# Attention scores as four quadrants of the matmul array: two heads on the rows, two halves of the queries on the columns

## The reference, cut to what matters

```
h = shift_token(x);  q, k, v = split(h @ wqkv);  q, k = l2norm(q) * qs, l2norm(k) * ksc
q, k = rotary_xpos(q, k)
bq = windows(q) * 8;  bk, bv = [previous window, own window] of k, v      # 128 queries, 256 keys
sim = einsum('bhwid,bhwjd->bhwij', bq, bk)
mask = (i < j) | (i > j + 128) | (j == -1)   # i, j: positions of query and key
out = softmax(where(mask, -max, sim)) @ bv;  x = x + out @ wo
```

## Time and profile before

| | |
|---|---|
| median of 3 runs | 977.15 us (977.08 to 978.51) |
| the profiled execution | 977.5 us, span 975.8 us |
| granted TensorE clock, mean | 0.993 |
| TensorE busy | 912.9 us (94%), 5688 matmuls |
| VectorE busy | 676.0 us (69%) |
| ScalarE busy | 514.0 us (53%) |
| GpSimd busy | 425.7 us (44%) |
| L1913, the scores, matmuls of 256 columns | 384, busy 47.9 us |
| L1913, matmuls of 128 columns | 128, busy 9.3 us |

### The profile page before, as it was taken

The page is one execution under the profiler, slowest core; times in us unless marked ns, Lnnn a source line. Parts: engine busy times, 40 slices in busy tenths (PEclk is TensorE's granted clock), DMA queues, the critical chain, the costliest instruction groups (busy, mean ns, idle before and its releaser), DMA issues.

```text
span 975.8 us, 17517 instructions
## 1 busy us (share of the span) xinstructions
PE 912.9 (94%) x5688; PEld 767.4 (79%) x5688; DVE 676.0 (69%) x1706; ACT 514.0 (53%) x1221; POOL 425.7 (44%) x420
## 2 busy tenths in 40 slices
PE   5999987999999969999999799999999999889998
PEld 4778875787878848888888688887888888768887
DVE  6889888476767686776767556677677766746563
ACT  5577830404040436767676634455767666654442
POOL 4432634022220386767676300007776767631110
PEclk9999998999999999999999999999999999999999
DMA  7202021000000000000001020000000000000001
GB/s 259 76 1 65 22 89 69 1 1 0 0 1 1 23 0 2 1 23 0 22 0 35 16 102 14 4 27 1 2 24 0 22 0 21 19 16 16 31 25 47
DMA packets 15716, 26.34 MB, mean 27 GB/s; under 512 B 1642, under 2 KB 12256, under 8 KB 14896
## 3 DMA queue, kind: packets, MB, share of 16 engines
q1 hardware_dynamic: 15664, 25.69, 8.0%
HBM read 20.53 MB, written 2.10 MB: 23 GB/s over the span
## 4 chain that ended last, share of the span: by engine, by line
PE 74%; DVE 11%; ACT 7%; issue 4%; POOL 3%; SPq 1%; DMA 1%; ACTq 0%; DVEq 0%; POOLq 0%
PE bank L1610 35%; PE bank L1959 5%; PE bank L1913 5%; PE bank L1937 5%; PE bank L1819 5%; PE bank L1923 4%; ACT probs L1477 3%; PE bank L1900 2%; PE bank L1782 2%; PE bank L1765 1%; DVE y L839 1%; DVE normed L1140 1%; PE bank L1947 1%; PE bank L2032 1%; PE bank L2029 1%
## 5 line engine op out<-in xcount | busy, mean ns | idle before, releaser
L1477 ACT ACTIVATE probs<-bank,row_min 128x256 f32<-128x256 f32 (+1 forms) x256 | 110.9, 457 | 119.5 <-DVE row_min L1065 119.5
L1065 DVE CUSTOM_DVE_ANT_0 bank<-bank,mask 128x256 f32<-128x256 f32 (+1 forms) x256 | 90.8, 431 | 5.7 <-PE bank L1913 5.6
L586 POOL TENSOR_TENSOR norms<-norms,minus_half 128x16 f32<-128x16 f32 x32 | 93.6, 2925 | 2.7
L1610 PE MATMUL bank<-wqkv_hi,x_hi 128*128 128x512 f32 x192 | 82.1, 428 | 1.9 <-DVE rot L1041 1.1
L1610 PE MATMUL bank<-wqkv_hi,x_lo 128*128 128x512 f32 x192 | 75.8, 395 | 0.0
L1610 PE MATMUL bank<-wqkv_lo,x_hi 128*128 128x512 f32 x192 | 75.2, 392 | 0.0
L1202 DVE SCALAR_TENSOR_TENSOR hidden<-bank,lcols,hidden 128x512 f32<-128x512 f32 (+1 forms) x48 | 36.0, 750 | 51.4 <-PE bank L1610 26.8
L568 POOL TENSOR_TENSOR q_tok<-rot 128x512 f32<-128x512 f32 x32 | 41.3, 1289 | 58.1 <-DVE rot L1041 58.1
L1923 PE MATMUL bank<-ident,probs 128*128 128x128 f32 x448 | 60.5, 276 | 3.9 <-ACT probs L1477 3.9
L1610 PE MATMUL bank<-t_hi,wm_lo 128*128 128x512 f32 x160 | 63.1, 394 | 0.0
L1959 PE MATMUL bank<-wo_sb,o_t 128*128 128x256 f32 x256 | 60.9, 381 | 2.3 <-DVE o_t L1080 1.7
(11 more groups left out here) (255 smaller groups left out, 2632.3 us busy)
## 6 DMA issues: line engine op xcount, KB each, us to landing
w_stage<-in_wm_l_dram SPq DMA_DIRECT2D x8, 534.0 KB, 3.6
w_stage<-in_wqkv_dram SPq DMA_DIRECT2D x2, 1536.0 KB, 7.7
out_dram<-stream SPq DMA_DIRECT2D x8, 256.0 KB, 2.4
emb<-in_ctx_dram SPq DMA_DIRECT2D x1, 1536.0 KB, 7.0
inner<-in_w_gate_dram SPq DMA_DIRECT2D x1, 1152.0 KB, 10.2
stream<-in_x_dram SPq DMA_DIRECT2D x2, 512.0 KB, 5.7
stream<-in_x_dram SPq DMA_DIRECT2D x1, 1024.0 KB, 12.7
ew<-in_pos_bias_dram SPq DMA_DIRECT2D x1, 1024.0 KB, 11.3
```

What stands on the lines that cost most here:

```text
L586: pool.tensor_tensor(norms[:, 2, :], norms[:, 1, :], minus_half[:, :], ALU.pow).then_inc(c_rn, 1)
L1065: dve.tensor_tensor_reduce(logits, logits, mask[:, 2 * P - nk:2 * P], 1.0, FAR, ALU.add, ALU.min, row_min[:, w % 2, 2 * i + e:2 * i + e + ...
L1477: act.activation(probs[:, i, e, 0:nk], logits, ACT.Exp, bias=row_min[:, w % 2, h:h + 1], scale=-1.0, accum_out=row_sum[:, w % 2, h:h + 1]) ...
L1610: ins = pe.matmul(out, stationary, moving, start=(first and i == 0), stop=(last and i == len(terms) - 1))
```

## The change

In windows with w > 0, each head's score matmul is split into two by queries: g = 0 has queries 0 to 63 as the stationary operand (64 x 64) and keys 0 to 191 as the moving one, and writes partitions 0 to 63; g = 1 has queries 64 to 127 and keys 64 to 255, and writes partitions 64 to 127, 64 columns further right. The two heads stay on the two halves of the array's rows, so the four matmuls of a pair of heads lie on its four quadrants. Places that no quadrant writes keep what the bank held; all of them are masked. In w = 0 windows the matmuls stay as they were. The semaphore is raised where it was. The waits for c_qt and c_pt_out go through `wait_alone`.

```diff
             def score_pairs(n, w):
 
-                pe.wait_ge(c_qt, n + 1)
+                wait_alone(pe, c_qt, n + 1)
                 k0 = max(w - 1, 0) * P
                 nk = (w + 1) * P - k0
                 for i in range(KI):
                     if i % 2 == 0 and not (isinstance(n, int) and n == 0):
-                        pe.wait_ge(c_pt_out, 4 * n - 2 + i)
-                    for e in range(2):
-                        half = slice(e * DH, (e + 1) * DH)
-                        ins = pe.matmul(bank[SCORES[i // 2] + e][:, (i % 2) * 2 * P:(i % 2) * 2 * P + nk],
-                                        q_t[half, i, :], k_t[half, i, k0:(w + 1) * P], start=True, stop=True)
+                        wait_alone(pe, c_pt_out, 4 * n - 2 + i)
+                    for g in range(2 if w else 1):
+                        for e in range(2):
+                            half = slice(e * DH, (e + 1) * DH)
+                            rows_out = slice(g * DH, (g + 1) * DH) if w else slice(0, P)
+                            nq = 3 * DH if w else P
+                            c0 = (i % 2) * 2 * P + g * DH
+                            ins = pe.matmul(bank[SCORES[i // 2] + e][rows_out, c0:c0 + nq], q_t[half, i, rows_out],
+                                            k_t[half, i, k0 + g * DH:k0 + g * DH + nq], start=True, stop=True)
                     if i % 2:
                         ins.then_inc(c_qk, 1)
```

## The result

The changed kernel takes 970.24 us (median of 4 runs, 969.63 to 971.49) against 977.83 for the kernel before in 4 runs of the same comparison: ratio 0.9914, 95% interval 0.9894 to 0.9933. The prediction was 970.0. The profiled execution took 969.63 us, with a span of 967.9, 7.9 us shorter than before.

What follows compares the result with a forecast made beforehand. TensorE was taken to bound the kernel nearly throughout. Per layer 2.76 + 0.50 + 0.20 + 0.08 = 3.54 us, for two layers 7.1, taken off the profiled 977.5 gave 970.4, against the median 970.05; predicted 970.0, range 968.8 to 971.4.

Steps and rivals of the forecast that it cites:

- The sum: Gains over all changed windows: 3.54 us per layer, 7.1 us for two layers.
- G: TensorE time saved in the block of scores per changed window: 1.92 - 1.46 = 0.46 us.
- The bound that had no row: Time of a group of four score matmuls: 0.157 us if all run together, 0.313 if column halves take turns; lower taken.
- Issue: 64 instead of 32 instructions pass TensorE's sequencer; the block wants 46 ns a pair, the trace shows about 20; taken as covered.
- rows 5: Trace rows at the start of layer 2: 16 score pairs within 0.33 us, about 20 ns each.
- The waits set apart: Three waits in the loop made instructions of their own: costed at nothing, range 0 to 0.25 us per window.
- What is late next: Chain from masks to queries' transposes: steady w = 2 and 3 windows gain 0.46 us each, w = 1 0.25.
- A: How much sooner the first half of a window's scores is ready for VectorE's masks: 0.25 us.
- The first and the last batch's w = 1 windows: Gain limited ahead of VectorE's first mask: first batch 0.08 us at most, last batch 0.20.
- The last w = 2 and 3 windows: Last batch, VectorE has other work ahead of the masks: gain 0, waits of 2.55 and 1.24 us grow about 0.46.
- Rivals 1 to 4: 973 us: only A kept (chance 0.13); 977: 59 ns pairs (0.07); 992: halves alternate (0.07); 966: all 24 keep G (0.03).

Runs made afterwards that it cites:

- e1: Kernel before with scores split into four quadrants, each half of the queries still taking all 256 keys; ratio 0.9996 to the kernel before.
- e4: Changed kernel with the two loops swapped, both query halves of one head first; 975.43 us in one run, block of scores 1.46 us.
- e2: Kernel before, unsplit, with 192 key columns instead of 256 in windows with w > 0; ratio 0.9944 to the kernel before.
- e3: Kernel before with only the three waits of the scores set apart as instructions; ratio 1.0004 to the kernel before.
- e6: Changed kernel with the next queries' transposes after all four quarters of the probabilities; 971.91 us, ratio 0.9921 to the kernel before.
- e7: Changed kernel with VectorE's MLP statistics moved after the masks in the last batch's w = 2 window; 970.45 us, ratio 0.9911 to the kernel before.
- e9: Changed kernel with filler matmuls, results unread, in two waits of each layer's last windows; 969.84 us, ratio 0.9914 to the kernel before.
- e8: Changed kernel with the queries' transposes last and VectorE's MLP statistics after the masks; 971.06 us, ratio 0.9907 to the kernel before.
- e5: The changed kernel again, unaltered, on the same chip as three later runs; 971.68 us, ratio 0.9919 to the kernel before.
- e10: Changed kernel with queries' transposes last, MLP statistics after the masks, and filler matmuls in the last windows' waits; 967.61 us, ratio 0.9892 to the kernel before.

## Why the prediction was right

- **The total.** The sum was 7.1 us; measured are 7.6 between the medians and 7.9 between the profiled executions. That 970.0 lies within 0.24 us of the median is partly luck: the sum started from the 977.15 of three runs, and with the fourth the median before is 977.83. These 0.7 us nearly cancel the 0.5 by which the gain was sized too small.
- **G, the block.** Predicted 1.46 us, measured 1.46. The bound that had no row, four quadrants in one group, fell to its lower end: e1 with 256 columns takes 1.89, so four cost what two do, and e4 shows that their order is free. The interpolation by columns holds: e2 measures 0.42 of it alone. (By the prediction's own rows 256 columns come to 2 x 0.83 / 8 = 0.2075 us, not 0.209; that moves the block by less than 0.01.)
- **Issue.** Covered, as rows 5 had said: 32 loads and 32 matmuls in 1.46 us are 46 ns a pair. The 62 ns on a matmul with hardware decode off, which the Trainium skill gives ("TensorE: Matmul & The Clock Gate", section "Wait — 56ns, not 53.3ns?"), are not this kernel's price.
- **The waits set apart.** Free: e3, and no step inside the block.
- **What is late next.** The w = 2 and 3 windows gained G, the w = 1 windows A = 0.25 (measured 0.26), because there the keys' copy still ended last. e6 confirms that by filling the wait, and shows that w = 0 windows hang on it too: a wait that I had passed over, because the listed idle time was small. In the w = 2 windows TensorE stays last, as forecast, but the room behind the keys' copy shrank from 0.51 to 0.42 us and not by G - A = 0.21: the copy begins 6.91 us after the first score instead of 7.32, sooner by 0.41 and not by A. Before the change it began 0.03 after TensorE had ended the keys' transposes, so it followed TensorE there and not ScalarE's chain; timeline of the kernel before, for the earlier trace rows:

```profile
440.65 0.60 PE L1892 MATMUL bank<-ident,k_tok 128*128 128x128 f32 x4
```

  One part of the expected picture was off: TensorE's idle time in the w = 1 windows is 12.38 - 12.23 = 0.15 us, not 0.33. The keys' transposes (L1892) come later as well, 5.51 us after the first score; before the change it was 5.82, less G would be 5.36. They wait for the keys that VectorE scales (L1056), which are done 0.15 us ahead of them (424.60 + 0.68 = 425.28 to 425.43, timeline of the kernel after):

```profile
424.60 0.68 DVE L1056 TENSOR_TENSOR k_tok<-k_tok,norms 128x512 f32<-128x512 f32 x1
```

  The listed end of the matmul before covers that gap.
- **The first and the last batch's w = 1 windows** were sized too small, 0.08 and 0.20 against 0.18 and 0.26. I had bounded them by VectorE's listed idle time; but the first mask starts 0.35 us after x_low's start, inside its listed 0.43 (371.07 and 371.42): listed lengths overlap there, so there was more room than the idle time says. Together that is 0.3 us more gain.
- **The last w = 2 and 3 windows** gained nothing, and their waits grew, as forecast: 2.55 to 3.00. In w = 2, e7 shows that VectorE's statistics ahead of the masks were the reason. What the prediction left out is that in some executions the clock falls at these waits. In the changed kernel's second profile this cost 1.1 and 2.3 us in the last w = 2 windows of the two layers. How much of it is in the median is not shown: e9, where the clock is whole there, has no better ratio.

Rivals 1 to 4 are out: the windows keep more than A, the pace is not 59 ns, no halves take turns, and the six windows outside the steady loop and the six w = 1 windows inside it did not keep G.

What stays open: how often the half clock comes in the last windows, and what brings it. That the wait's growth from 2.55 to 3.00 us does is not shown. One of two profiles of the changed kernel had it there; of the kernel before and of e1 and e3, with waits of 2.54 to 2.58 us, none had. But e2, with waits of 2.97, had none either, and e7 and e8 had it after waits of only 2.09 and 2.23. So the length of the wait alone does not decide.

## What to carry to other kernels

A block of matmuls on parts of the array was priced here by the columns that each member streams, from two blocks of different width in the trace; the split itself was free, so it pays where it lets columns be left out. Sort the places where a saving lands by who ends last there, and count the full saving only where the engine fills its window; elsewhere count what the chain behind it gains. Where a saving only lengthens an idle time, look at the granted clock there, in more than one profile: where the clock fell at such a wait, it cost 1.1 and 2.3 us in e5, more than the 0.46 us that the change saves in a window that TensorE fills, and a single profile can miss it.

## What the runs showed of the hardware

- Four fp32 matmuls on the four quadrants, each with moving data of its own, run together and take no longer than two on the row halves: 1.46 us for 8 groups of four with 192 columns and 1.89 with 256 (e1), against 1.50 (e2) and 1.92 for 8 groups of two.
- In the last w = 2 windows, where TensorE idles 2.1 to 3.0 us, the granted clock fell to half in 8 of the 14 windows in the profiles of e2, e4 to e8 and the change, and in none of the 6 of the kernel before, e1 and e3. With filler matmuls in the waits it stayed whole there in all four of e9 and e10.
